# Attention's steps in another order: a third weighted-value buffer, one-hots a step earlier, query products further forward

## The chip, the cores and the metric

One Trainium2 chip, one core. The metric is the time of one execution on the device in microseconds, the median of several runs. The kernel before has 2334.35 us (three runs, 2334.18 to 2335.04).

## What is computed

Four graph layers over 3125 nodes with 128 features and 53125 edges sorted by their target node: a relational layer with 16 relations, a two-stage relational layer with 32 relations and tanh, a plain sum layer with relu, and an attention layer with 8 heads of 16. After each stands a residual sum and a layer norm. The change touches the attention alone:

```python
q = (h @ Wq + bq).reshape(n, OUT_DIM, H) * scaling
k = (h @ Wk + bk).reshape(n, OUT_DIM, H)
v = (h @ Wv + bv).reshape(n, OUT_DIM, H)
s = jnp.einsum('edh,edh->eh', q[row], k[col])
m = jax.ops.segment_max(s, row, num_segments=n)
p = jnp.exp(s - m[row])
z = jax.ops.segment_sum(p, row, num_segments=n)
attn = p / z[row]
out = jax.ops.segment_sum(attn[:, None, :] * v[col], row, num_segments=n)
```

Here row is the target of an edge and col its source.

## The kernel before, in words

The first three layers come first (some 1700 us), and while the third one ends, the table of keys and values (`kv_d`, 256 floats a node) and the table of queries (`q_d`, in three bf16 parts) are written to device memory. Then function `attention` runs. It works on 416 chunks of 128 edges. Four chunks are a group (`QC = 4`, numbered q, 104 of them), sixteen chunks or four groups are a batch (`KB = 26` batches, numbered k). Every engine runs its own list of instructions, written out by hand as one loop over steps; the engines meet through semaphores only, and each engine works strictly down its list. In step k an engine handles the batch that is entering ("now", k), the one whose scores are complete ("mid", k - 1) and the one whose weights are complete ("old", k - 2).

GpSimd has one loop (L1338): for each chunk an indirect DMA gathers 128 rows of `kv_d` into one of 64 places of `G`, four batches deep. Every eighth gather waits first until the product with the weights of the chunk that held its place is done (`s_pv`). SyncE loads the query windows (`QW`, eight of them, L1309), each when the query product eight groups back is done, and stores finished tiles (L1314).

What an edge goes through, group by group or batch by batch:

- **One-hots.** VectorE compares each edge's target, relative to its group's first node, with 0 to 39 (`one_hots`, L1602, four instructions a batch, bf16). ScalarE writes each of these three times side by side (`thrice`, L1483), TensorE transposes them (`one_hot_rows`, L1359, one group a time through the one PSUM tile `p_oh`), and ScalarE copies the result out (`one_hot_copy`, L1490).
- **Query products.** TensorE multiplies the transposed one-hots by the query window, which puts each edge's query on its row (`queries`, L1369, into two PSUM tiles in turn; it waits for the key product two groups back).
- **Key products and scores.** VectorE multiplies them by the gathered keys (`products`, L1609, reads PSUM and `G`), sums within heads (`head_part`, L1615) and adds the batch's sums to the scores (`head_sums`, L1622).
- **Maxima per node.** TensorE transposes the batch's scores (`scores_t`, L1415); VectorE runs two scans along edges (`chunk_max`, L1626 and L1627); TensorE moves the end columns into a row (`rows`, L1375 and L1376), ScalarE copies it out (`rows_copy`), VectorE scans across the chunks and makes three small copies (`row_max`, L1640 to L1647), ScalarE orders the result (`rows_ordered`), TensorE makes columns of it (`columns`, L1380), ScalarE copies those (`columns_copy`), and VectorE scans again with these starts (`segment_max`, L1626 to L1656).
- **Weights.** ScalarE takes the exponential (`weights`, L1515), TensorE transposes back (`weights_back`, L1397), ScalarE copies out (`weights_copy`, L1521, into `ps`). `difference`, `fade_log`, `fade` and `rescale` correct the one node that runs on from batch to batch.
- **Node sums.** VectorE multiplies gathered values by the weights (`values`, L1676, into `PV`, two buffers; group q waits until the node sum of group q - 2 is done) and makes the fp32 one-hots (`window_factors`, L1663). TensorE multiplies the two (`window_sums`, L1406 and L1409, into two PSUM tiles), VectorE adds them to the sums (`add`, L1703).
- **Outputs.** For a tile of 128 nodes whose edges are through, TensorE transposes the sums (`output_t`), VectorE divides, adds the residual and takes the norm's statistics (`outputs`, L1709 to L1720), ScalarE takes a root (`deviation`, L1531), VectorE normalises (`normalise`, L1728). From step 4 on nearly every step carries one tile, the last step two; steps 1 to 3 and 11 carry none.

VectorE's order in a step, which is what the change edits most:

```python
products(4k-1), head_part(4k-1), head_sums(k-1)
values(4k-6), rescale(k-2), add(4k-8)
chunk_max(k-1)
products(4k), head_part(4k)
outputs, row_max(k-1), one_hots(k+1)
add(4k-7), values(4k-5)
products(4k+1), head_part(4k+1), segment_max(k-1), add(4k-6), normalise
products(4k+2), head_part(4k+2), add(4k-5)
window_factors(k-1), fade_log(k-1), values(4k-4), values(4k-3)
```

## Time and profile before

| | |
|---|---|
| median of three runs | 2334.35 us |
| the profiled execution, by its own time | 2332.2 us |
| its span, first to last instruction | 2330.3 us |
| TensorE matmul busy | 1670.3 us (72%) |
| TensorE weight loads busy | 1238.1 us (53%) |
| VectorE busy | 1539.0 us (66%) |
| ScalarE busy | 435.6 us (19%) |
| GpSimd busy | 1636.8 us (70%) |
| first and last start of the attention's gathers | 1728.6 and 2286.4 us |
| granted TensorE clock, mean; in the attention | 0.611; 0.50 |

The profile shows one execution. Busy time counts what an engine executes, not its waits. In the timeline a row gives start, duration, engine, operation and line, tiles and shapes, and in brackets how long the engine sat idle before it and what ended that; "issue" means that nothing the profile sees was waited for. Consecutive instructions of one kind are merged into a row with their count (x4), whose duration runs from the first's start to the last's end.

### The profile page before, as it was taken

How to read it: one execution, taken by the hardware profiler on the slowest of the kernel's cores; microseconds unless marked ns; L12 is line 12 of the kernel's file. 1: busy time of each engine (PE TensorE's matmuls, PEld its weight loads, DVE VectorE, ACT ScalarE, POOL GpSimd, SP SyncE). 2: the span in 40 equal slices, each digit the busy share in tenths (PEclk: the TensorE clock that was granted, in tenths of full speed). 3: DMA queues.
4: the chain of work that ended last, by engine and by line, in shares of the span. 5: the costliest groups of instructions: out<-in, count | busy, mean ns of one | idle time of the engine just before them, and what ended most of it. 6: DMA issues, size and time to landing. Idle time of an engine off the chain costs nothing. (4 is left out here: it accounts for less than half of the span.)

```text
span 2330.3 us, 32319 instructions
## 1 busy us (share of the span) xinstructions
PE 1670.3 (72%) x8464; PEld 1238.1 (53%) x8464; DVE 1539.0 (66%) x5260; ACT 435.6 (19%) x994; POOL 1636.8 (70%) x1687
## 2 busy tenths in 40 slices
PE   4877777765766766775567667667957888888886
PEld 3655555553555555554444444444426667677775
DVE  8776776665666666664355555556657787788785
ACT  0000000002000000002111111111343343344342
POOL 6777777775777777775777777774227777777772
PEclk9975555555556665555587777787555555555555
DMA  5233233232233233235232332332423333333331
GB/s 139 56 85 83 57 85 84 56 84 70 56 84 84 85 84 112 56 84 155 54 98 83 98 99 83 98 99 82 80 87 107 105 108 106 108 105 107 108 104 36
DMA packets 149656, 207.12 MB, mean 89 GB/s; under 512 B 48936, under 2 KB 111387, under 8 KB 149360
## 3 DMA queue, kind: packets, MB, share of 16 engines
q0 software_dynamic: 61280, 138.20, 22.1%
q1 hardware_dynamic: 87186, 65.12, 9.5%
q10 hardware_dynamic: 1010, 1.73, 0.2%
q8 instruction: 73, 1.20, 0.2%
q14 instruction: 107, 0.88, 0.1%
HBM read 172.14 MB, written 36.04 MB: 89 GB/s over the span
## 5 line engine op out<-in xcount | busy, mean ns | idle before, releaser
L507 POOL DMA_INDIRECT G<-h_d,idx x832 | 794.6, 955 | 283.9 <-issue 261.8
L570 PE MATMUL p_g<-S,G 128*128 128x96 f32 (+1 forms) x2496 | 609.0, 390 | 462.6 <-DMA G<-h_d,idx 300.7
L570 PEld LDWEIGHTS p_g<-S,G 128*128 128x128 f32 x2496 | 526.6, 292 | 667.2 <-issue 295.0
L1338 POOL DMA_INDIRECT G<-kv_d,idx x416 | 432.4, 1039 | 201.8 <-issue 201.8
L507 POOL DMA_INDIRECT G<-in_x,idx x416 | 397.6, 956 | 132.2 <-issue 119.4
L928 DVE TENSOR_SCALAR work<-iota_h,key_f 128x600 bf16<-128x600 f16 x416 | 171.0, 411 | 253.9 <-PE p_d L581 253.6
L903 DVE SCALAR_TENSOR_TENSOR S<-con,rel,shared 128x96 f32<-128x96 f32 (+1 forms) x1248 | 315.4, 293 | 0.5
L581 PE MATMUL p_d<-work 128*128 128x312 bf16 (+1 forms) x832 | 272.2, 428 | 18.0 <-DVE work L943 17.1
L921 DVE TENSOR_TENSOR agg<-agg,p_g 128x96 f32 (+1 forms) x624 | 143.7, 230 | 104.1 <-PE p_g L570 84.3
L1406 PE MATMUL p_w<-S,PV 128*128 128x40 f32 x832 | 199.2, 415 | 0.7 <-DVE PV L1676 0.7
L943 DVE TENSOR_TENSOR work<-work,p_d 128x312 f32 (+1 forms) x416 | 190.8, 459 | 10.4 <-issue 9.6
L1406 PEld LDWEIGHTS p_w<-S,PV 128*128 128x128 f32 x832 | 186.6, 329 | 15.9 <-issue 10.8
L1019 DVE TENSOR_TENSOR work<-work,p_d 128x512 f32<-128x512 f32 (+1 forms) x168 | 104.3, 625 | 137.1 <-PE p_d L616 136.6
L616 PE MATMUL p_d<-work,q_s 128*128 128x512 bf16 (+1 forms) x525 | 161.0, 429 | 1.9 <-DVE q_s L1008 0.9
L581 PEld LDWEIGHTS p_d<-work 128*128 128x128 bf16 x832 | 116.6, 163 | 34.8 <-DVE work L929 18.1
L1359 PE MATMUL p_oh<-idb,ohn 128*120 128x128 bf16 x416 | 68.9, 321 | 75.8 <-ACT ohn L1483 43.0
L1615 DVE TENSOR_REDUCE hs<-XH 128x32 f32<-128x512 f32 x104 | 111.6, 1073 | 3.5
L705 ACT ACTIVATE xt_s<-p_xt 128x128 f32<-128x128 f32 x75 | 20.8, 278 | 488.8 <-PE p_xt L592 488.8
L929 DVE TENSOR_SCALAR work<-iota_h,lo_f 128x128 bf16<-128x128 f16 x416 | 109.6, 263 | 0.0
L1359 PEld LDWEIGHTS p_oh<-idb,ohn 128*120 128x120 bf16 x416 | 51.9, 213 | 93.0 <-ACT ohn L1483 56.6
L1609 DVE TENSOR_TENSOR XH<-p_qe,G 128x512 f32<-128x512 f32 x104 | 70.8, 681 | 45.7 <-DMA G<-kv_d,idx 35.6
L1676 DVE TENSOR_TENSOR PV<-G,ps 128x512 f32<-128x512 f32 x104 | 68.9, 684 | 20.8 <-PE p_w L1409 20.8
(253 smaller groups left out, 2093.3 us busy)
## 6 DMA issues: line engine op xcount, KB each, us to landing
work<-A_d SPq DMA_DIRECT2D x25, 800.0 KB, 4.5
A_d<-work SPq DMA_DIRECT2D x12, 1600.0 KB, 7.5
G<-h_d,idx POOLq DMA_INDIRECT x832, 2.5
G<-in_x,idx POOLq DMA_INDIRECT x416, 2.5
G<-kv_d,idx POOLq DMA_INDIRECT x416, 2.8
h_d<-XH SPq DMA_DIRECT2D x75, 64.0 KB
h_d<-in_x SPq DMA_DIRECT2D x2, 1600.0 KB, 7.4
kv_d<-kv_s SPq DMA_DIRECT2D x25, 128.0 KB, 1.7
```

What stands on the lines that cost most here:

```text
L507: pool.indirect_dma_start(G[:, c % GRING, :], None, l.table, bass.IndirectOffsetOnAxis(ap=l.places[:, c:c + 1], axis=0)).then_inc(s_arr[g ...
L570: last = pe.matmul(p_g[:, g % PB, 0:width], G[:, c % GRING, :], S[:, c % (SRING * GR), 0:width], start=(k == 0), stop=(k == GR - 1))
L581: last = pe.matmul(p_d[:, 1 + half, 0:(hi - lo) * W], lows[:, slot, :], keys[:, slot, lo * W:hi * W], start=(k == 0), stop=(k == GR - 1))
L616: last = pe.matmul(p_d[:, n % 3, 0:width], q_s[:, t % QS, k, :], A_s[:, t % AB, cols], start=(k == 0), stop=(k == QR - 1))
L903: last = dve.scalar_tensor_tensor(S[:, slot + k, 0:l.nb * W].rearrange("p (b w) -> p b w", w=W), bc(iota, 1, l.nb), rel[:, c:c + 1], bc(co ...
L921: dve.tensor_tensor(place, place, p_g[:, g % PB, 0:l.nb * W].rearrange("p (b w) -> p b w", w=W), ALU.add).then_inc(s_added, 1)
L928: dve.tensor_scalar(keys[:, slot, :], iota_h[:], key_f[:, c:c + 1], None, ALU.is_equal)
L943: dve.tensor_tensor(place, place, p_d[:, 1 + half, 0:(hi - lo) * W].rearrange("p (t w) -> p t w", w=W), ALU.add).then_inc(s_bad, 1)
L1338: pool.indirect_dma_start(G[:, c % KRING, :], None, d["kv"], bass.IndirectOffsetOnAxis(ap=idx[:, c:c + 1], axis=0)).then_inc(s_ar[c // QC ...
L1359: last = pe.matmul(p_oh[0:QR * WA, c * P:(c + 1) * P], ohn[:, k % 2, j * QC + c, :], idb[:], start=True, stop=True)
L1406: pe.matmul(p_w[:, q % 2, 0:WA], PV[:, q % 2, c, :], S01[:, j * QC + c, :], start=(c == 0), stop=(c == QC - 1))
L1615: dve.tensor_reduce(hs[:, j * QC:(j + 1) * QC, :], prod[:, j * QC:(j + 1) * QC, :].rearrange("p c (d h) -> p c h d", h=HEADS), AX_X, ALU.a ...
```

## The change

It gives `PV` a third buffer, so that the product of group q waits for the node sum of group q - 3; issues the one-hots of a batch one step earlier (VectorE gets a step -2 for this, and the last real step that issues any is 23); moves `products(4k)` ahead of `chunk_max(k-1)` on VectorE; on TensorE moves `scores_t(k-1)` and `queries(4k)` ahead of `window_sums(4k-7)` and `queries(4k+2)` ahead of `columns(k-1)`; and on ScalarE moves the four `thrice` of a step forward, two of them to its start. The number of instructions of each kind stays.

```diff
+VRING = 3
-    PV = sb("PV", [P, 2, QC, D])
+    PV = sb("PV", [P, VRING, QC, D])
     STEPS = range(-1, KB + 3)
+    DVE_STEPS = range(-2, KB + 3)
@@ TensorE, window_sums
-                    pe.matmul(p_w[:, q % 2, 0:WA], PV[:, q % 2, c, :], S01[:, j * QC + c, :], start=(c == 0),
+                    pe.matmul(p_w[:, q % 2, 0:WA], PV[:, q % VRING, c, :], S01[:, j * QC + c, :], start=(c == 0),
@@ TensorE, the steps
                     if old:
                         window_sums(4 * k - 8)
-                        window_sums(4 * k - 7)
                     if mid:
                         scores_t(k - 1)
                     if now:
                         queries(4 * k)
+                    if old:
+                        window_sums(4 * k - 7)
+                    if now:
                         queries(4 * k + 1)
                     if mid:
                         rows(k - 1)
                     if old:
                         window_sums(4 * k - 6)
+                    if now:
+                        queries(4 * k + 2)
                     if mid:
                         columns(k - 1)
-                    if now:
-                        queries(4 * k + 2)
                     if nxt:
                         one_hot_rows(4 * k + 4)
@@ ScalarE, the steps
                     mid, nxt = batch(k - 1), batch(k + 1)
+                    if nxt:
+                        thrice(4 * k + 4)
+                        thrice(4 * k + 5)
                     if mid:
                         penalties(k - 1)
                         rows_copy(k - 1)
...
                     for t in in_step(k - 1):
                         deviation(t)
                     if nxt:
-                        thrice(4 * k + 4)
-                        thrice(4 * k + 5)
+                        thrice(4 * k + 6)
+                        thrice(4 * k + 7)
                         one_hot_copy(4 * k + 4)
                     if mid:
                         weights(k - 1)
                     if nxt:
-                        thrice(4 * k + 6)
-                        thrice(4 * k + 7)
                         one_hot_copy(4 * k + 5)
@@ VectorE, values
-                if q >= 2:
-                    dve.wait_ge(s_mm, q - 1)
-                dve.tensor_tensor(PV[:, q % 2].rearrange("p c (d h) -> p c d h", h=HEADS),
+                if q >= VRING:
+                    dve.wait_ge(s_mm, q - VRING + 1)
+                dve.tensor_tensor(PV[:, q % VRING].rearrange("p c (d h) -> p c d h", h=HEADS),
@@ VectorE, the steps
-                for k in STEPS:
+                for k in DVE_STEPS:
...
                         add(4 * k - 8)
+                    if now:
+                        products(4 * k, landed)
                     if mid:
                         chunk_max(k - 1)
                     if now:
-                        products(4 * k, landed)
                         head_part(4 * k)
                     for t in in_step(k - 1):
                         outputs(t)
                     if mid:
                         row_max(k - 1)
-                    if nxt:
-                        one_hots(k + 1)
+                    if batch(k + 2):
+                        one_hots(k + 2)
```

## Rows read from the trace of the kernel before

**Rows 1.** The page's costliest groups: busy us, mean ns, idle time before them.

```profile
L1338 POOL DMA_INDIRECT G<-kv_d,idx x416 | 432.4, 1039 | 201.8 <-issue 201.8
```

**Rows 2.** Source view of the gathers, duration in ns: min/median/max, first and last start.

```profile
L1338 POOL DMA_INDIRECT G<-kv_d,idx x416: 942/947/2127, 1728.6 to 2286.4; - x139
```

**Rows 3.** Waits, 1740 to 2330: us in total, times, longest.

```profile
POOL G L1338 <- issue: 124.0, 407, 0.3
...
DVE XH L1609 <- DMA G<-kv_d,idx: 35.6, 46, 2.4
...
DVE PV L1676 <- PE p_w L1409: 20.8, 23, 2.1
```

**Rows 4.** Timeline of one batch (13), GpSimd and VectorE: start us, duration us, what.

```profile
2007.05 1.50 POOL L1338 DMA_INDIRECT G<-kv_d,idx  x1 [0.30 <-issue]
...
2011.35 0.94 POOL L1338 DMA_INDIRECT G<-kv_d,idx  x1 [0.30 <-issue]
...
2011.75 0.69 DVE L1676 TENSOR_TENSOR PV<-G,ps 128x512 f32<-128x512 f32 x1 [0.86 <-PE p_w L1409]
...
2015.23 0.67 DVE L1609 TENSOR_TENSOR XH<-p_qe,G 128x512 f32<-128x512 f32 x1
...
2018.84 1.11 POOL L1338 DMA_INDIRECT G<-kv_d,idx  x1 [0.30 <-issue]
...
2019.46 1.01 DVE L1602 TENSOR_TENSOR oh<-con,rel 128x160 bf16<-128x160 f32 x4
...
2020.26 1.79 POOL L1338 DMA_INDIRECT G<-kv_d,idx  x1 [0.30 <-issue]
...
2020.55 0.67 DVE L1676 TENSOR_TENSOR PV<-G,ps 128x512 f32<-128x512 f32 x1
...
2022.35 0.94 POOL L1338 DMA_INDIRECT G<-kv_d,idx  x1 [0.30 <-issue]
...
2025.15 0.69 DVE L1609 TENSOR_TENSOR XH<-p_qe,G 128x512 f32<-128x512 f32 x1 [0.15 <-DMA G<-kv_d,idx]
...
2028.70 1.50 POOL L1338 DMA_INDIRECT G<-kv_d,idx  x1 [0.30 <-issue]
```

**Rows 5.** Timeline of batch 4, GpSimd and VectorE.

```profile
1817.09 0.96 POOL L1338 DMA_INDIRECT G<-kv_d,idx  x1 [0.30 <-issue]
1817.12 0.70 DVE L1676 TENSOR_TENSOR PV<-G,ps 128x512 f32<-128x512 f32 x1 [0.59 <-PE p_w L1409]
...
1819.95 0.42 DVE L1626 TENSOR_TENSOR_SCAN FB<-shared,p_sT 128x128 f32<-128x128 f32 x1 [1.37 <-PE p_sT L1415]
...
1820.60 0.67 DVE L1609 TENSOR_TENSOR XH<-p_qe,G 128x512 f32<-128x512 f32 x1
...
1824.62 0.95 POOL L1338 DMA_INDIRECT G<-kv_d,idx  x1 [0.30 <-issue]
...
1824.89 1.01 DVE L1602 TENSOR_TENSOR oh<-con,rel 128x160 bf16<-128x160 f32 x4
...
1825.87 1.60 POOL L1338 DMA_INDIRECT G<-kv_d,idx  x1 [0.30 <-issue]
1825.98 0.67 DVE L1676 TENSOR_TENSOR PV<-G,ps 128x512 f32<-128x512 f32 x1
```

**Rows 6.** Timeline of the last batch's maxima, TensorE and VectorE.

```profile
2290.38 1.93 PE L1406 MATMUL p_w<-S,PV 128*128 128x40 f32 x8
...
2292.25 0.29 DVE L1622 TENSOR_TENSOR SC<-SC,hs 128x128 f32<-128x128 f32 x1
...
2292.88 0.48 PE L1415 MATMUL p_sT<-con,SC 128*128 128x128 f32 x1
...
2294.48 0.59 PE L1375 MATMUL p_sm<-con,FB 128*1 128x128 f32 x2 [1.13 <-DVE FB L1627]
```

**Rows 7.** Timeline early in the attention.

```profile
1763.91 1.01 DVE L1602 TENSOR_TENSOR oh<-con,rel 128x160 bf16<-128x160 f32 x4
1763.94 1.80 POOL L1338 DMA_INDIRECT G<-kv_d,idx  x1 [0.30 <-issue]
```

## The prediction, made before the changed kernel ran

> **What bounds the kernel now.** The change lies in the attention alone, so I first asked the page's costliest groups who works through that part. The gathers of keys and values lead: 416 of them, 432.4 us busy, and before each only idle time that nothing explains, 201.8 us in all [rows 1]. The source view adds that half of them last 947 ns [rows 2]. The list of waits of the attention says the rest: GpSimd waits for nobody, 124.0 us in 407 gaps of at most 0.3 us [rows 3], so a plain gather costs 0.95 + 0.30 = 1.25 us and sixteen, one batch, 20.0 us. VectorE's products instead wait 35.6 us for gathers to land [rows 3]. The first loop is the bound, VectorE follows it. That decides what waits are worth: those that the change attacks (20.8 us of the weighted-value product for the node sums, the largest of them [rows 3]) end on an engine that has to wait for a gather later in the same batch.
>
> But a batch takes more than 20.0 us. From the first gather of batch 13 (2007.05) to that of batch 14 (2028.70) it is 21.65 us, because a few gathers are long [rows 4]. Over all 416: 432.4 - 416 x 0.947 = 38.5 us. The timeline of VectorE and GpSimd together shows where. The tenth of a batch lasts 1.11 us, the eleventh 1.79 us, the first of the next 1.50 us [rows 4]. The eleventh starts at 2020.26, inside the four one-hot comparisons (2019.46 to 2020.47), and ends at 2022.05, which is 0.83 us after the weighted-value product behind them ends (2020.55 + 0.67 = 2021.22) [rows 4]. In 19 of the 26 batches a gather of 1.78 or 1.79 us stands behind the one-hots. So what can move the time is **where VectorE's instructions on two SBUF inputs fall on the starts of gathers**, and that is a matter of some tenths of a microsecond, batch after batch.
>
> A page of the Trainium skill would weigh this differently. "SBUF — State Buffer", section "Who interferes with whom", says that a tensor-by-tensor operation takes only the read side of the port pair shared with GpSimd and that descriptor generation needs the write side, which it calls inferred. By that the product could not lengthen a gather and no shift of it could gain anything (the no-gain rival below); the end 0.83 us behind the product, in 19 batches, speaks against it. The same section has the pair locked for a whole instruction by whoever starts first; yet the product of 2011.75 starts 0.40 us into a gather, and both keep their usual 0.69 and 0.94 us [rows 4].
>
> **The change part by part.**
> Three buffers: values(4k-6) waits for node sums three back, long done. It starts its 0.86 us of waiting earlier, at 2010.89 in place of 2011.75 [rows 4]. Gain in time: nothing, VectorE next needs the gathers of group 4k. Its end, about 2011.54, lies 0.19 us past the start of the batch's fourth gather (2011.35); with 0.82 us from a release to a gather's end this makes 1.01 for that gather, 0.06 longer. Bounds 0 and 0.16 (the excess of the tenth in [rows 4]); I take 0.04 x 20 = 0.8 us in all.
>
> Products of group 4k ahead of chunk_max: this is the term that counts. Its last gather, the fourth, starts at 2011.35. Where VectorE waits for a landing, the product starts 2.80 us after the last gather's start (2022.35 to 2025.15) [rows 4]. So it will start at 2014.15 in place of 2015.23, and now VectorE does wait there. TensorE is ready: the query product no longer stands behind a second node sum of 2.50 us (2290.38 to 2292.88, [rows 6]). Behind the product come the two scans, which take 0.65 us of VectorE (1820.60 - 1819.95 in the batch of [rows 5], whose first scan stands just before its product). head_part then starts at 2014.15 + 0.70 + 0.65 = 2015.50, not 2015.93: **all up to the product of group 4k+1 comes 0.43 us earlier against the gathers**.
> What that does to them the trace already shows. In batch 4 the product of group 4k started 3.51 us after the fourth gather (1817.09 to 1820.60), in the usual batch 3.88 (2011.35 to 2015.23): 0.37 us earlier. There the tenth gather lasts 0.95 us, although the one-hots start 0.27 us after it, and the eleventh 1.60 us, as the product starts 0.11 after it [rows 5]. Batch 12 repeats this. The sum of the two excesses is 0.66 instead of 1.00. With another 0.06 us of shift the product ends at +0.72, the eleventh lasts 1.54: I take 0.38 us saved per batch. Bounds: 0 and 1.00 (both excesses gone). Fifteen batches of the usual pattern: 5.7 us. Batch 8, whose eleventh is the longest with 2127 ns [rows 2], some 0.7; batch 24, in which the one-hots are no longer issued, all of 1.0; the others (2, 3, 11, 18, 25) 0.6 together. That is 8.0 us.
>
> The second collision (the first gather, 0.55 us a batch) stays. It hangs on the product of group 4k+2, which waits 0.15 us for its gathers at 2025.15 [rows 4]. The twelfth moves 0.38 earlier, VectorE 0.43 earlier; it still waits, about 0.2. If that cover went, the pair would slide by some tenths: bounds -0.6 and +0.6 per batch, taken 0.
>
> One-hots a step ahead: as many as before. Those of batch 1 move to where VectorE waits for the first query products; 0. On ScalarE the tripled one-hots move to the start of the step, where it waits for the row maxima, so that two of them no longer stand between the weights and their copy back; the products with these weights stand behind VectorE's own window factors and fade_log, so 0. If that cover went, the weights would come earlier, not later: no loss. SyncE's window loads wait for query products, which come earlier; GpSimd's queue is untouched, its wait for free key buffers never showed.
>
> TensorE's order in the last batch costs. Nothing follows there, so every position shows. Today the second node sum (from 2290.38) runs while VectorE finishes the last scores (2292.25 + 0.29 = 2292.54), the transpose follows at 2292.88, the rows of maxima at 2294.48, when the scans are ready [rows 6]. Afterwards TensorE idles for the scores, transposes at 2292.59, and then the second node sum stands ahead of the rows: 2292.59 + 0.3 + 2.5 = 2295.4, against 2294.48 now. The row scans, the ordered columns and the weights all wait for them in turn: **0.9 us lost**. Bounds 0 (if other work hides it) and 2.5, one node sum.
>
> **Sum**: -8.0 + 0.8 + 0.9 = -6.3 us. The profiled execution took 2332.2 us (span 2330.3), which gives 2325.9; the median of the runs is 2.15 us above it, so 2334.35 - 6.3 = 2328.0 us. About 0.2%, 4.7 us, is what a measurement of this kernel can tell from no change.
>
> **Rivals.**
> 1. The eleventh gather gets free. The one-hots would end 0.05 us before its start and the product start 0.03 after it. In batch 4 a product that starts 0.03 us into a gather, 1817.12 at 1817.09, leaves it at 0.96 us [rows 5]. Then 20 x 0.62 = 12.4 us more go: 2315.6. But VectorE comes too late for its second wait and the second collision slides, up to 0.5 x 20 back: 2315 to 2326. For: my shift lies 0.05 beyond the known one. Chance 0.15.
> 2. No net gain. The shift is smaller than worked out or the excess moves to another gather (released at the one-hots' end it would be 1.08 in one gather, as much as today), and 0.9 is lost at the end: 2335 to 2337. Chance 0.25.
> 3. Slower: the tenth gather is caught. Early in the attention a gather that starts at 1763.94, 0.03 us into the one-hots, lasts 1.80 us, until all four are over [rows 7]. After the change they start at 2019.46 - 0.43 = 2019.03, 0.19 us behind the tenth gather. Were it held through one-hots and product (to 2020.79 + 0.82), it would last 2.77 us, an excess of 1.82 against 1.00: 20 x 0.82 + 0.9 = +17.3, 2351.7. It decides where the one-hots start no later than the gather, 0.19 us from my working; batch 4, with 0.27 us, was free [rows 5]. Chance 0.12. By the page's section named above the small copies ahead of the one-hots would lock the pair as well; read so, this rival would be the likely one.
> 4. VectorE is the bound after all and its removed waits count: 2334.35 - 20.8 = 2313.6. Against it stand all waits for gathers. Chance 0.03.
>
> My forecast has 0.45. Around it the copying of batch 4's figures gives 2323 to 2332, of which some 0.7 lies below 2329.7. Faster: 0.32 + 0.15 + 0.03 = 0.50. Slower: 0.14, the third rival and a rest of the second. Same: 0.36. The range runs from 2315 to 2339 and leaves out the third rival and the lowest part of the first.
>
> **What would show it.** The product for node sums three back without a wait; products of group 4k that start 2.8 us after the fourth gather and wait 1 to 2 us for it; tenth gathers of 0.95 and elevenths of 1.5 to 1.6 us; the first gather of a batch still 1.50; a period of some 21.3 us; in the last batch the rows of maxima late by 0.9 us. Elevenths of 0.95, tenths above 2 us, or a first gather far from 1.50 would prove the sum wrong, and a GpSimd that waits for a VectorE semaphore the whole reading.

## The result and the profile after

The changed kernel takes 2341.8 us (median of 11 runs, 2338.05 to 2346.0) against 2334.3 us (11 runs) for the kernel before in the same comparison: ratio 1.0033, 95% interval 1.0024 to 1.0043. It is slower by 7.5 us where 6.3 us less had been forecast, and outside the range. The profiled execution has 2340.63 us with a span of 2338.7 us, 8.4 us more than before. The third rival happened, in half of the batches. One thing is needed to read the numbers below: in the comparisons of e1 to e4, f1, g1, k1, k2 and l1 the kernel before itself took 2975 to 3035 us, so these can't be laid beside the others.

The page's costliest groups after, with busy time, mean ns and idle time before them, answer to [rows 1]:

```profile
L1340 POOL DMA_INDIRECT G<-kv_d,idx x416 | 439.2, 1056 | 202.4 <-issue 202.4
...
L1614 DVE TENSOR_TENSOR XH<-p_qe,G 128x512 f32<-128x512 f32 x104 | 71.4, 686 | 105.8 <-DMA G<-kv_d,idx 95.2
```

The waits from 1740 us to the end, after (us in total, times, longest), answer to [rows 3], and the source view of the gathers (ns min/median/max, first and last start) to [rows 2]:

```profile
POOL G L1340 <- issue: 124.3, 408, 0.3
DVE XH L1614 <- DMA G<-kv_d,idx: 95.2, 68, 2.8
```

```profile
L1340 POOL DMA_INDIRECT G<-kv_d,idx x416: 942/946/2759, 1729.7 to 2294.3; - x139
```

Everything that the change was to take away is gone: no product for node sums waits for TensorE any more. GpSimd still waits for nobody. But the same 416 gathers are busy 6.8 us longer (439.2 against 432.4 [rows 1]); the median gather is unchanged and the longest grew from 2127 to 2759 ns [rows 2]. VectorE's wait for landings grew from 35.6 to 95.2 us: what it saved it now spends waiting for slower gathers.

From the first to the last start of a gather it is 564.6 us, before 557.7: that is 6.9 of the 8.4 us of span. Another 1.0 us lies ahead of the attention (first gather 1729.69 against 1728.65). It is no part of the change: of the experiments below, one that has all of before's order starts at 1733.2. The last 0.6 us is behind the last gather.

The timeline of batch 14 after, VectorE and GpSimd, shows where a gather grows (it answers to batch 13 in [rows 4]):

```profile
2036.38 0.95 POOL L1340 DMA_INDIRECT G<-kv_d,idx  x1 [0.30 <-issue]
...
2039.19 0.69 DVE L1614 TENSOR_TENSOR XH<-p_qe,G 128x512 f32<-128x512 f32 x1 [2.08 <-DMA G<-kv_d,idx]
2039.80 0.41 DVE L1631 TENSOR_TENSOR_SCAN FB<-shared,p_sT 128x128 f32<-128x128 f32 x1
...
2040.43 1.05 DVE L1620 TENSOR_REDUCE hs<-XH 128x32 f32<-128x512 f32 x1
...
2043.79 0.15 DVE L1651 COPY R<-R 1x8 f32<-1x8 f32 x1
...
2043.87 2.65 POOL L1340 DMA_INDIRECT G<-kv_d,idx  x1 [0.30 <-issue]
...
2043.94 1.01 DVE L1607 TENSOR_TENSOR oh<-con,rel 128x160 bf16<-128x160 f32 x4
...
2045.03 0.67 DVE L1681 TENSOR_TENSOR PV<-G,ps 128x512 f32<-128x512 f32 x1
```

The product of group 4k starts 2.81 us after the fourth gather (2036.38), as forecast, and waits 2.08 us for it, a little over the 1 to 2 us forecast. The tenth gather (2043.87) starts 0.07 us before the four one-hots, ends at 2046.52, and that is 0.82 us after the product for the node sums is over (2045.03 + 0.67 = 2045.70): held through four one-hots, a sum and a product. In batch 17 the one-hots come 0.27 us behind the tenth, and it is free; batch 24 has no one-hots at all, and the tenth is free though a product starts 0.16 us into it:

```profile
2111.09 0.95 POOL L1340 DMA_INDIRECT G<-kv_d,idx  x1 [0.30 <-issue]
2111.20 0.15 DVE L1651 COPY R<-R 1x8 f32<-1x8 f32 x1
...
2111.36 1.01 DVE L1607 TENSOR_TENSOR oh<-con,rel 128x160 bf16<-128x160 f32 x4
...
2112.34 1.60 POOL L1340 DMA_INDIRECT G<-kv_d,idx  x1 [0.30 <-issue]
```

```profile
2266.05 0.95 POOL L1340 DMA_INDIRECT G<-kv_d,idx  x1 [0.30 <-issue]
2266.21 0.68 DVE L1681 TENSOR_TENSOR PV<-G,ps 128x512 f32<-128x512 f32 x1
```

Sorted by that offset, the 26 batches tell where the time went (excess is the time of a batch's gathers above 0.947 us each, in us and summed over the batches of the row):

| batches | one-hots start after the tenth gather by | tenth, eleventh, us | excess after | the same batches before |
|---|---|---|---|---|
| 4, 6-9, 14-16, 18-22 (13) | 0.07 to 0.18 us | 2.65-2.76, 0.95 | 31.5 | 20.9 |
| 5, 11, 12, 17, 23 (5) | 0.27 to 0.37 | 0.95, 1.60-1.71 | 6.9 | 7.7 |
| 10, 13 (2) | 0.74 to 0.77 | 0.95, 2.08-2.11 | 3.6 | 3.3 |
| 24, 25 (2) | none issued | 0.95, 0.95 | 1.3 | 2.4 |
| 0 to 3 (4) | start-up | | 2.0 | 4.0 |

Together +6.8 us: thirteen caught batches cost 10.6, the rest gains 3.8.

The end, from the timeline of the last batch after (to [rows 6]):

```profile
2300.07 0.29 DVE L1627 TENSOR_TENSOR SC<-SC,hs 128x128 f32<-128x128 f32 x1
...
2300.41 0.47 PE L1417 MATMUL p_sT<-con,SC 128*128 128x128 f32 x1 [2.12 <-DVE SC L1627]
...
2302.38 0.70 PE L1411 MATMUL p_w<-S,ps 128*8 128x40 f32 x8
...
2302.88 0.42 PE L1377 MATMUL p_sm<-con,FB 128*1 128x128 f32 x1
```

The rows of maxima start 2.52 us after the scores are complete (2300.36), before it was 1.94 (2294.48 against 2292.54 [rows 6]): 0.58 us lost, with the node sum between the scores and them, as forecast in kind.

### The profile page after: what moved, and what is told of

It reads as the page before. It is cut to its first block and busy times, and to the rows that moved or that the text cites. A ratio compares the mean times of both kernels' runs of the same rounds, so it can differ in the third digit from the quotient of the medians.

```text
span 2338.7 us, 32318 instructions
## 1 busy us (share of the span) xinstructions
PE 1671.4 (71%) x8464; PEld 1240.2 (53%) x8464; DVE 1531.9 (66%) x5260; ACT 432.6 (18%) x994; POOL 1643.7 (70%) x1687
## 5 line engine op out<-in xcount | busy, mean ns | idle before, releaser
L1340 POOL DMA_INDIRECT G<-kv_d,idx x416 | 439.2, 1056 | 202.4 <-issue 202.4
L1408 PE MATMUL p_w<-S,PV 128*128 128x40 f32 x832 | 197.8, 414 | 0.9 <-DVE PV L1681 0.8
L1614 DVE TENSOR_TENSOR XH<-p_qe,G 128x512 f32<-128x512 f32 x104 | 71.4, 686 | 105.8 <-DMA G<-kv_d,idx 95.2
L706 ACT ACTIVATE xt_s<-p_xt 128x128 f32<-128x128 f32 x75 | 20.8, 277 | 484.1 <-PE p_xt L593 484.1
L617 PEld LDWEIGHTS p_d<-work,q_s 128*128 128x128 bf16 x525 | 60.4, 124 | 39.5 <-issue 16.6
```

Of the source, the lines that this page charges most:

```text
L617: last = pe.matmul(p_d[:, n % 3, 0:width], q_s[:, t % QS, k, :], A_s[:, t % AB, cols], start=(k == 0), stop=(k == QR - 1))
L1340: pool.indirect_dma_start(G[:, c % KRING, :], None, d["kv"], bass.IndirectOffsetOnAxis(ap=idx[:, c:c + 1], axis=0)).then_inc(s_ar[c // QC ...
L1408: pe.matmul(p_w[:, q % 2, 0:WA], PV[:, q % VRING, c, :], S01[:, j * QC + c, :], start=(c == 0), stop=(c == QC - 1))
```

## The experiments

**Delay, and one part undone.** e1_delay puts one more instruction ahead of row_max in the kernel after:

```diff
+    idle = sb("idle", [P, 200])
...
                     if mid:
+                        dve.memset(idle[:], 0.0)
                         row_max(k - 1)
```

i1_delay is the same kernel. e2 and i2 (onehots_early) move the one-hots of the kernel after to where VectorE waits for gathers:

```diff
                         add(4 * k - 8)
+                    if batch(k + 2):
+                        one_hots(k + 2)
                     if now:
                         products(4 * k, landed)
...
-                    if batch(k + 2):
-                        one_hots(k + 2)
```

g1 and i3 (before_onehots_early) do the like in the kernel before:

```diff
+                    if nxt:
+                        one_hots(k + 1)
                     if mid:
                         chunk_max(k - 1)
...
-                    if nxt:
-                        one_hots(k + 1)
```

e3 and i4 (scans_first) undo VectorE's swap in the kernel after:

```diff
-                    if now:
-                        products(4 * k, landed)
                     if mid:
                         chunk_max(k - 1)
                     if now:
+                        products(4 * k, landed)
                         head_part(4 * k)
```

> The kernel after, with one more VectorE instruction a step: a spare tile's 200 columns set to zero ahead of row_max, 0.2 to 0.25 us. Theory A (the tenth gather of 13 batches is caught, 2.7 us, because the one-hots start up to 0.18 us after it): the one-hots now start 0.3 to 0.45 us after the tenth, which gets 0.95 us, the eleventh gets 1.6 to 1.8; about 1 us less in 13 batches, 2326 to 2334 us in spite of the added work. Theory B (VectorE's order or load makes the attention longer): 2342 to 2348.

2331.8 us (ratio to before 0.9991, 0.9981 to 1.0000), 10 us less than the kernel after, **with one instruction more in every step**. Theory B, a price of the order or of VectorE's load, falls. Twice in its trace, batch 14 and batch 22:

```profile
2044.47 0.95 POOL L1341 DMA_INDIRECT G<-kv_d,idx  x1 [0.30 <-issue]
...
2044.60 0.15 DVE L1652 COPY R<-R 1x8 f32<-1x8 f32 x1
...
2044.75 1.01 DVE L1608 TENSOR_TENSOR oh<-con,rel 128x160 bf16<-128x160 f32 x4
```

```profile
2216.06 0.15 DVE L1652 COPY R<-R 1x8 f32<-1x8 f32 x1
2216.07 2.73 POOL L1341 DMA_INDIRECT G<-kv_d,idx  x1 [0.30 <-issue]
...
2216.21 1.01 DVE L1608 TENSOR_TENSOR oh<-con,rel 128x160 bf16<-128x160 f32 x4
```

With the one-hots 0.28 us behind it the tenth is free, with 0.14 it is held. Over the whole run a gather was held at offsets up to 0.18 us (seven batches, in two of them it was the eleventh) and free from 0.27 us. The delay did not free all, since VectorE's place within the batch also varies.

> The kernel after, with one_hots(k+2) ahead of products(4k), where VectorE waits for gathers. Nothing is added. Theory A: the tenth and eleventh meet at most a single product (excess 0.6 at most), the one-hots catch the gather that starts just before or inside them, about the fifth, held to 0.82 us after the four are over (excess 0.3 to 0.9): 2318 to 2332. Theory B (the added waits and moved products themselves): 2340 to 2343.

2315.1 us (0.9919, 0.9905 to 0.9933), 3 us under the low end. From batch 3 on no tenth or eleventh gather is long; the gathers take 28.6 us less than in the kernel after. The page's costliest groups, and the timeline of the new place in batch 16:

```profile
L1340 POOL DMA_INDIRECT G<-kv_d,idx x416 | 410.6, 987 | 204.7 <-issue 204.7
```

```profile
2067.44 1.02 DVE L1607 TENSOR_TENSOR oh<-con,rel 128x160 bf16<-128x160 f32 x4
2068.01 1.03 POOL L1340 DMA_INDIRECT G<-kv_d,idx  x1 [0.31 <-issue]
```

That the fifth gather starts in the midst of the four one-hots and takes 1.03 us is better than theory A allowed: held to their end it would have had 0.45 + 0.82 = 1.27. I had not expected it, and the last measurement below is about it.

> The kernel before, with one_hots(k+1) moved ahead of chunk_max(k-1) and nothing else. Theory A: the run of four one-hots and a product is taken apart; what is behind chunk_max comes at the same place, the tenth and eleventh meet a single product; 2316 to 2332. Theory B (the one-hots' place doesn't matter to the gathers): 2333 to 2337.

2330.95 us (0.9986, 0.9977 to 0.9995). It lies within the expectation, but for another reason. The gathers are free, more than in i2 (406.4 us busy); but VectorE no longer keeps up. The distance from the fourth gather of a batch to its product grows from 4.8 us (batch 4) to 27.0 (batch 25), and its wait for a free PV buffer grows from 20.8 us [rows 3] to 48.4. **There is a second bound besides the gathers.**

> The kernel after, with chunk_max(k-1) ahead of products(4k) again. Theory A: the run comes back by 0.4 us to where it was before, one-hots past the tenth gather by 0.5 to 0.6 us, tenth 1.0 to 1.1 and eleventh 1.8: 2333 to 2337. Theory B (the loss comes from three buffers, one-hots a step ahead or TensorE's order): 2339 to 2343.

2337.1 us (1.0014, 1.0005 to 1.0024), 0.1 us above the range of theory A, and not by the way I had given: I had the one-hots back at 0.5 to 0.6 us behind the start of the tenth gather. In most batches the tenth gather starts 0.46 us into the one-hots and is held to 0.82 us behind the end of the product. My earlier expectation for e3, the same kernel (below), had just this: one-hots some 0.5 us ahead of the tenth, tenth 2.0 to 2.1.

```profile
2108.97 1.01 DVE L1607 TENSOR_TENSOR oh<-con,rel 128x160 bf16<-128x160 f32 x4
2109.43 2.12 POOL L1340 DMA_INDIRECT G<-kv_d,idx  x1 [0.30 <-issue]
...
2110.05 0.67 DVE L1681 TENSOR_TENSOR PV<-G,ps 128x512 f32<-128x512 f32 x1
```

The gathers are busy 436.1 us, between before (432.4) and after (439.2), and the time lies between too. So undoing the swap gives back 4.7 of the 7.5 us. What is left is again a matter of the offset: the excess of most batches is 1.9 us, against 1.6 before.

**The buffer alone, and the second bound.** j2 has the third buffer alone; j4 adds i3's edit to it; j3 is i2 with one product moved:

```diff
                     if mid:
                         products(4 * k - 1, landed)
+                    if old:
+                        values(4 * k - 7)
+                    if mid:
                         head_part(4 * k - 1)
...
                         values(4 * k - 4)
-                        values(4 * k - 3)
```

> The kernel before with the third weighted-value buffer alone. My own term for it was +0.8 us. Theory A (only the start of VectorE's runs against the gathers counts; the product of values then starts up to 0.86 us earlier, the one-hots stay): 2333 to 2337 us. Theory B (the buffer itself makes the loss): 2339 to 2343.

2335.05 us (0.9999, 0.9990 to 1.0008): nothing, where I had reckoned 0.8 us. The 20.8 us of wait for node sums [rows 3] are gone from VectorE and stand before its first scan instead, which waits for the transposed scores: 31.7 us in the kernel before, 52.8 us here (waits of 1740 us to the end; of the run with the buffer alone, one line):

```profile
DVE FB L1627 <- PE p_sT L1416: 52.8, 24, 2.5
```

TensorE does both node sums ahead of those scores, so the sum of the two waits stays.

> The kernel before with two edits: three weighted-value buffers, and one_hots(k+1) ahead of chunk_max(k-1). With the second alone (2330.95 us) the gathers were free, 13 us over the plain 0.95 in all, and VectorE fell behind, waiting for node sums in front of its products for PV. Theory C (that wait for a buffer is what bounds it): the third buffer takes it away, VectorE keeps up with the gathers: 2310 to 2320. Theory D (VectorE's and TensorE's own work bounds it): 2328 to 2332.

2329.2 us (0.9974, 0.9965 to 0.9983). Theory C falls: the buffer was not what held VectorE back. Its products of group 4k stand in the timeline 21.66 us apart, here in batches 17 and 18, while the gathers run ahead with 20.4 us a batch:

```profile
2099.65 0.67 DVE L1610 TENSOR_TENSOR XH<-p_qe,G 128x512 f32<-128x512 f32 x1
...
2121.31 0.67 DVE L1610 TENSOR_TENSOR XH<-p_qe,G 128x512 f32<-128x512 f32 x1
```

The chain of waits of this kernel, 2112 to 2124 us (start, duration, what), shows through what:

```profile
2115.23 1.86 PE p_w L1407 x8
2117.09 0.63 PE p_w L1410 x8
2117.72 1.86 PE p_w L1407 x8
2119.58 0.63 PE p_w L1410 x8
2120.22 0.42 PE p_sT L1416
...
2120.66 0.42 DVE FB L1627
...
2121.31 0.68 DVE XH L1610
```

Two node sums of 2.5 us each, then the transposed scores, the scans, the product. The kernel before has the same ring, and no gather lies on it: from batch 4 on none of its products of group 4k waits for a landing, and they start 21.65 to 21.69 us apart in 19 of 21 cases, while the gathers' period varies from 21.28 to 21.75 us. From the product of its batch 13, 2015.23 in [rows 4], the ring runs through the row scans, ScalarE, the transposed one-hots and the node sums to the product of batch 14, 21.66 us behind:

```profile
2019.23 0.43 ACT L1505 ACTIVATE R<-R 1x128 f32<-1x128 f32 x1 [2.39 <-DVE R L1641]
...
2023.32 0.68 PE L1359 MATMUL p_oh<-idb,ohn 128*120 128x128 bf16 x4 [1.82 <-ACT ohn L1483]
...
2030.74 1.93 PE L1406 MATMUL p_w<-S,PV 128*128 128x40 f32 x8
...
2036.24 0.42 DVE L1626 TENSOR_TENSOR_SCAN FB<-shared,p_sT 128x128 f32<-128x128 f32 x1 [1.38 <-PE p_sT L1415]
...
2036.89 0.67 DVE L1609 TENSOR_TENSOR XH<-p_qe,G 128x512 f32<-128x512 f32 x1
```

VectorE's waits for gathers in between (0.15 us at 2025.15 [rows 4], 0.96 us later) don't reach TensorE: the product for the node sum at 2030.74 is over at 2029.37. So in the kernel before the ring sets the pace, and its gathers, 21.65 us a batch, are hardly as long as that by accident: the later VectorE's run stands against the tenth gather, the longer this gather gets (1.06 us at an offset of 0.57, 1.12 at 0.63), so that gathers which run ahead are held back. This link is argued from the rows, not tested. Free gathers alone bring little (3.3 us in i3, 5.5 in j4); in i2, which has the change's order as well, they bring 19.

> The kernel after with the one-hots early (2315.1 us), and the second of the two weighted-value products at the step's end moved behind the first products of the next step. Theory A: the first gather of a batch no longer meets a run of fp32 one-hots and two products; it gets 0.95 instead of 1.50, another one meets the moved product (excess 0.2 to 0.6); VectorE still waits for gathers: 2303 to 2315. Theory C (with so few long gathers VectorE is at its own bound, 20.6 us a batch): 2313 to 2320, its waits for gathers gone and the distance from gather to product growing from batch to batch.

2308.4 us (0.9885, 0.987 to 0.990), the fastest of all and ahead of both kernels by 26 and 33 us. From batch 4 on the first gather has 0.95 us in thirteen batches, 1.0 to 1.13 in seven and 1.4 in two, where it had 1.50; the third took 1.0 to 1.3 instead in most, and VectorE still waits for landings (58.3 us), so theory C falls. Its 416 gathers are busy 404.0 us.

**Which part takes the ring away** was still open: k1 (l1 is the same kernel) adds TensorE's order of the kernel after to j4, k2 the swap as well.

```diff
                         window_sums(4 * k - 8)
-                        window_sums(4 * k - 7)
                     if mid:
                         scores_t(k - 1)
                     if now:
                         queries(4 * k)
+                    if old:
+                        window_sums(4 * k - 7)
+                    if now:
                         queries(4 * k + 1)
...
```

> The kernel before with three weighted-value buffers and the one-hots ahead of chunk_max (2329.2 us, gathers free, VectorE falling behind by 1.25 us a batch: a batch takes it 21.66 us), and now TensorE's order of the kernel after. Theory E (a ring bounds it that runs over the second node sum ahead of scores_t, the scans, the scores' sums, row_max, the columns, the transposed one-hots and back to the node sums): taking the 2.5 us node sum out of it lets VectorE keep pace with the gathers, 2308 to 2318 us. Theory F (VectorE's own work, or TensorE's, in whatever order): 2326 to 2332.

> As the run before it, and products(4k) ahead of chunk_max(k-1) too; what is left out of the change is the one-hots' extra step and ScalarE's order. Theory E: the ring is broken already, the swap moves nothing by itself: within 4 us of the run before it. Theory G (it is the swap that frees VectorE): the run before it stays at 2326 to 2332 and this one has 2308 to 2318. Theory H (the one-hots' extra step or ScalarE's order does it): both stay at 2326 to 2332.

> The same kernel as k1: three weighted-value buffers and the one-hots ahead of chunk_max in the kernel before (2329.2 us with these two), and TensorE's order of the kernel after. Theory E (the ring over the second node sum ahead of scores_t bounds the attention once the gathers are free; TensorE's order takes it out): 2308 to 2318 us. Theory F (VectorE's or TensorE's own work, or the swap, or the one-hots' extra step): 2326 to 2332.

2960.1, 2958.5 and 2960.5 us beside 2980.2 and 2977.6 of the kernel before: ratios 0.9932 (0.9908 to 0.9956), 0.9927 (0.9900 to 0.9953), 0.9933 (0.9911 to 0.9956). They say that the swap adds nothing to TensorE's order there. But in these comparisons GpSimd waited for VectorE (197.8 us for PV in k1), so gathers and ring don't meet as they do at 2334 us. Which part of the change's order takes the ring away stays open: theory E is argued from the chain above, not shown.

The other runs of that kind: e1_delay 3007.3 (ratio 1.0102, 1.0076 to 1.0128) and its repeat f1_delay 3006.7 (1.0096), e2_onehots_early 2978.6 (0.9986), e3_scans_first 2999.6 (1.0073), e4_three_buffers_only 2993.2 (1.0052), g1_before_onehots_early 3041.7 (1.0017, 0.9995 to 1.0039). They had been expected as follows, in this order:

> The changed kernel with one more VectorE instruction a step, a memset of 200 columns (some 0.2 us) ahead of the row scans; nothing is left out. Theory A, the gather that is caught: in the changed kernel the one-hots start 0.07 to 0.18 us behind the start of the tenth gather, which then lasts 2.65 to 2.76 us, while batches with 0.27 to 0.37 us have a tenth of 0.95 and an eleventh of 1.60 to 1.71. With 0.2 us more work the one-hots start 0.27 to 0.38 us behind it, so the tenth is free in all batches, a batch's excess falls from 2.4 to some 1.3 us, and the kernel gets FASTER by adding work: about 2327 us (2324 to 2331). Theory B, the order makes VectorE wait longer for gathers (95 us against 36 us) and so makes the batch longer: more work on VectorE can only cost, 2342 to 2347 us.

> The same kernel as in e1_delay, repeated, because in that call the kernel before itself took 2977 us instead of 2334 and the gathers there waited for other engines (240 us for VectorE's weighted-value products), so that they were not the bound. If the kernel before takes its 2334 us again, the expectations stand as for e1_delay. Theory A (the tenth gather is caught by the one-hots if they start up to 0.18 us behind it): 0.2 us more work on VectorE a step frees the tenth gather in all batches and the kernel gets faster than the changed one, about 2327 us (2324 to 2331), against 2341.8. Theory B (VectorE's work and waits count): 2342 to 2347 us.

> The changed kernel with the one-hots of the batch after next moved from between the row scans and the add to ahead of the products of group 4k, where VectorE waits some 2.2 us for gathers. Nothing is left out. Theory A: the run of one-hots, add and product is what holds the tenth gather; batches 24 and 25 of the changed kernel, which issue no one-hots, have a tenth and an eleventh of 0.95. So both are free in all batches, the first stays 1.50, and the fourth or fifth gather, whose start may now fall into the one-hots, gets up to 0.4 us longer. Excess 0.6 to 1.0 us a batch: 2310 to 2322 us. Theory B: the waits for gathers stay as long or the sum of VectorE's work stays the same, so about 2342 us.

> The changed kernel with one part undone: on VectorE the products of group 4k stand behind the chunk maxima again. Nothing is left out. Theory A: the products still wait for the gathers at the same place, but the scans are done before, so all that follows comes 0.65 us earlier than in the changed kernel: the one-hots start some 0.5 us ahead of the tenth gather and the product ends 1.25 us behind its start; tenth 2.0 to 2.1 us, ninth some 1.1, excess about 1.85 a batch against 2.4 now and 1.64 before: 2334 to 2340 us, slower than before and a little faster than the changed one. Theory B: with this part undone VectorE is as before or freer, at most 2334 us.

> The kernel before with the third weighted-value buffer alone. Nothing is left out. Theory A: VectorE's product for the third group of the old batch comes 0.9 us earlier and VectorE waits later instead; the chunk maxima still wait for TensorE, so the run of one-hots meets the tenth and eleventh gather as before; the fourth gather may get 0.0 to 0.1 longer: 2333 to 2337 us. Theory B, VectorE's waits count: some of the 20.8 us go, 2314 to 2330 us.

> The kernel before with its one-hots moved, in the same step, from between the row scans and the add to ahead of the chunk maxima, where VectorE waits 1.4 to 1.6 us for the transposed scores. Nothing else changes, nothing is left out. Theory A (the run of one-hots, add and product holds the eleventh gather): the add and the product now follow the row scans at once, the product ends about as the eleventh gather starts, and that gather is free (0.95 in place of 1.79); the tenth keeps up to 0.16 over, the first its 1.50, and the sixth gather, whose start may fall into the moved one-hots, gets up to 0.2 longer. Excess of a batch 0.8 to 1.0 in place of 1.64 us: 24 x 0.7 = 17 us faster, 2312 to 2322 us where the kernel before takes 2334. Theory B (VectorE's work decides, not where it falls on the gathers): its work is the same and its waits get shorter by the hidden one-hots, but GpSimd's time a batch stays: 2334 us, no change. Where the kernel before takes 2975 us, as in the last two calls, with TensorE stalled for up to 32 us by nothing that the profile shows, neither has a clear price: up to 1.0 us a batch less on VectorE's chain, 2950 to 2980.

None of these is a test of theory A. GpSimd waited for other engines (257.4 us for PV in g1), and the kernel after was not among these runs, so that e1, e2, e3 and f1 have the kernel before alone beside them. Moving the one-hots of the kernel before gained nothing there (g1); why the buffer alone cost 0.5% (e4), where it cost nothing in j2, is open.

**The offset measured by itself.** h1 and j1 have no layers, only back-to-back gathers and, in every trial, VectorE's run after a delay that grows from trial to trial. In short, the second pair of sets of j1:

```diff
+                    dve.memset(p_x[:, 0:100 + STEP * i], 0.0)
+                    dve.tensor_tensor_scan(...)
+                    dve.tensor_copy(...)    # three
+                    onehots(oh1)
+                    dve.tensor_tensor(agg[:], agg[:], p_w[...], ALU.add)
+                    value(slot)
```

> A kernel of its own: it leaves the whole computation out and writes a copy of x. GpSimd gathers back to back, eight gathers a trial; in each of 4 x 26 trials VectorE waits until four gathers have landed, sets some columns of a spare tile to zero (59 more from trial to trial, about 0.05 us each, so that the rest falls on all parts of a gather in turn) and then runs: in the first 26 trials two short scans, three copies, four one-hots, the sum from PSUM, a weighted-value product and a key product; in the next 26 the same without one-hots; in the third the weighted-value product alone; in the last four fp32 one-hot instructions and two weighted-value products. Theory A (a gather is lengthened if a run of VectorE's instructions on two SBUF inputs is at work when it starts, and then lasts to about 0.82 us after that run ends): gathers last 0.95 us unless the run is at work within some 0.2 us of their start; in the first set the longest reach 2.7 us, namely where the one-hots start up to 0.18 us after the gather or up to about 0.2 us before; where they start 0.27 us or more after it the gather keeps 0.95 and the next one has 1.6 to 2.1. Set 2 and 3: at most about 1.5 to 1.7 us. Theory B (the gathers' length in the attention comes from something else, such as DMA load or the waits of VectorE's order): gathers of 0.95 us at every offset, or lengthened evenly.

The delay was itself a write to SBUF, and it held gathers too, up to 3.35 us in the third set where I had expected 1.7 at most. The starts of gathers were thereby pushed to the same place in most trials (in the first set 0.60 us into the one-hots), and the window of interest stayed empty. Of use is only that a hold may go through several instructions and ends 0.82 us behind the last of them; the key product that followed, which reads PSUM, did not prolong it.

> A kernel of its own as in the first measurement of offsets; it leaves the whole computation out and writes a copy of x. Now the delay is a write to PSUM (100 columns and 33 more from trial to trial; every second set with 600 columns ahead of it), to see whether gathers are left alone by it and the run behind it falls on every part of a gather. Four pairs of sets: (1) a scan, three copies and the four one-hots, nothing behind them; (2) the same with the sum and a weighted-value product behind them, as in the attention; (3) the product alone; (4) one-hots, sum and product with no copies ahead. Theory A: a gather that starts less than about 0.2 us before the run, or inside it, is held to 0.82 us after the run's end; one that starts over 0.25 us before it keeps 0.95. So in (2) and (4) the longest gathers have 2.6 to 2.8 us and the jump from 0.95 lies between 0.18 and 0.27 us; in (3) at most 1.5 to 1.7. Theory A2 (the hold ends at a border between two instructions if the gather asks at that moment): in (1) many gathers inside the one-hots end at 1.0 or less. Theory B: no jump at any offset.

Now the window is full. Two neighbouring trials of the second set, and one of the fourth, in which no copies precede the one-hots:

```profile
727.38 0.28 DVE L258 COPY RB<-R 1x8 f32<-1x8 f32 x3
727.41 2.76 POOL L215 DMA_INDIRECT G<-kv_d,idx  x1 [0.30 <-issue]
727.58 1.01 DVE L234 TENSOR_TENSOR oh<-con,rel 128x160 bf16<-128x160 f32 x4
```

```profile
739.22 0.95 POOL L215 DMA_INDIRECT G<-kv_d,idx  x1 [0.30 <-issue]
739.24 0.32 DVE L258 COPY RB<-R 1x8 f32<-1x8 f32 x3
739.48 1.01 DVE L234 TENSOR_TENSOR oh<-con,rel 128x160 bf16<-128x160 f32 x4
```

```profile
1857.47 1.08 DVE L234 TENSOR_TENSOR oh<-con,rel 128x160 bf16<-128x160 f32 x4
1857.72 0.94 POOL L215 DMA_INDIRECT G<-kv_d,idx  x1 [0.30 <-issue]
```

The step is sharp: in the first two sets all 26 gathers that started from 0.31 us after the first one-hot's start to 0.17 us before it were held to 0.82 us behind the run (1.6 to 2.0 us without the product, 2.3 to 2.76 with it), and all ten that started 0.26 to 0.29 us before it had 0.95. Between the two trials shown 0.09 us of offset is 1.81 us in length. What lies there is the three copies, the first of which starts 0.19 to 0.28 us ahead of the one-hots. Gathers that started earlier still, under the write to PSUM and the scan, had up to 1.87 us and ended 0.82 us behind the scan. Twice I was wrong. Without the copies, in the fourth set, I had expected 2.6 to 2.8 us; gathers that started inside the one-hots were let in between two of them, 0.94 to 1.09 us. In the third set gathers took up to 2.20 us, since the write to PSUM held them as well.

## Why the prediction was wrong

**What bounds the kernel**: right for the kernel after, not for the kernel before. After the change the time follows the long gathers (+6.9 of +8.4 us), and from batch 4 on VectorE waits for a landing ahead of every product of group 4k. But before it, "The first loop is the bound, VectorE follows it" overlooked VectorE's ring with TensorE, 21.66 us, which keeps its time without a gather on it. That GpSimd waits for no semaphore does not make the length of its gathers its own: they were held by VectorE. This is not what missed the number, since the change's order takes the ring away too; but by it the fourth rival deserved more thought.

**"Three buffers ... 0.8 us in all"**: 0 (j2, 0.9999). In after the fourth gather keeps 0.94 to 0.95 in most batches.

**"Products of group 4k ahead of chunk_max: this is the term that counts"** is the step that failed. Its mechanism held: product 2.81 us after the fourth gather, the run behind it earlier. Two things in it were off.

First the size of the shift. I let head_part start 0.70 + 0.65 = 1.35 us after the product's start. In the trace it is 1.24 (2039.19 to 2040.43): the 0.70 is the distance from product to head_part, but a scan starts 0.61 us after it, inside the product's recorded duration. The shift was 0.54, not 0.43 us, and the one-hots came 0.07 us behind the tenth gather (0.07 to 0.18 in the thirteen batches) where I had 0.19.

Second, and heavier, the precedent. "What that does to them the trace already shows" took batch 4, offset 0.27, for an offset of 0.19, with the nearest caught gather 0.03 us on the other side [rows 7]. The step lies between 0.18 and 0.27 us, so even 0.19 was no safe side of it, and an error of 0.1 us turned -0.38 us a batch into +0.81 in thirteen batches. I called it "it decides where the one-hots start no later than the gather"; in truth it decides 0.2 us earlier: by j1 the step lies where row_max's small copies begin, the first of them 0.23 us ahead of the one-hots in batch 14. The five batches that by chance had about batch 4's offset (0.27 to 0.37) did in kind what I forecast: tenth 0.95, eleventh 1.60 to 1.71, where I had 1.54.

**The rule of the Trainium skill.** The traces show a hold that begins among the small copies, up to 0.18 us ahead of the one-hots. The Trainium skill, "SBUF — State Buffer", section "Who interferes with whom", says that a copy within SBUF can take the port pair shared with GpSimd and that whoever issues first has it: by that the third rival was the likely one, as the prediction says in its last sentence on it, and I gave it 0.12. The same section's other statement, that a tensor-by-tensor operation leaves descriptor generation alone (inferred, it says), the runs contradict: in the third set of j1 gathers that start up to 0.5 us into a product, with nothing behind it, end 0.82 us after it.

**The second collision stays**: right, the first gather has 1.50 us in 20 of the 22 batches from 4 on.

**"0.9 us lost"** at the end: 0.58. I took 2.5 us for the node sum; from its start (2300.68) to the rows (2302.88) it is 2.20, since the rows start inside its recorded duration.

**The moved one-hots, the tripled ones, SyncE and GpSimd at nothing**: nothing in the trace speaks against it, though the one-hots' extra step was not run alone.

**The sum** then: thirteen batches +10.6, five and two of other offsets -0.6, the last two -1.1, the first four -2.0, the end +0.6, a start 1.0 later that is none of the change's: 8.5 of 8.4 us. The third rival's price (0.82 us a batch) was right to 0.01, its count 13 in place of 20, its condition off by 0.2 us, its chance too small.

## What to carry to other kernels

Where a time hangs on how two engines' instructions fall on each other within some tenths of a microsecond, an offset worked out to 0.1 us does not tell the side of a step: price both sides, and let the chance follow the distance to the nearest rows on each. Better still, take the collision out: put the run that holds the other engine where its own engine waits anyway (in the kernel after this took off 27 us, and 33 with a product moved as well). But the same move in the kernel before took off 3 us, because a ring of waits of 21.66 us a batch stood behind gathers of 21.65: before counting a bound's loss as a gain, look for the next bound. And an engine that waits for no semaphore can still be held by another, so its busy time does not prove it the bound.

## What the runs showed of the hardware

- An indirect gather of 0.95 us that starts during a back-to-back run of VectorE (one-hots, sum and product; a product alone; zeros and a product) can be held until 0.82 us behind its end, up to 2.76 us in the attention and 3.35 us in h1; a product that starts 0.40 us into a gather does nothing to it [rows 4].
- Three copies of 8 numbers on one partition, of 0.15 us each, can begin such a run, and with them ahead the four one-hots hold a gather as one block. With a write to PSUM (j1) or a sum (i2) ahead in their place, gathers were let in between two one-hots (0.94 to 1.09 us). Why the copies close those gaps is open.
- Writes of zeros held gathers too, to SBUF (h1) and, in front of a product or a scan, to PSUM (j1).
- In batches 24 and 25 of the kernel after a product 0.16 and 0.26 us behind the gather's start did no harm, with the small copies and a sum ahead (0.95 and 0.96 us, though in batch 25 the gather starts amid the copies); behind one-hots a product at 0.10 us did (batch 17, 1.60 us). What decides between these was not measured.
